# Half of the transposes, or a statistics product, placed ahead of the next product A

## What is computed

```
x = x + L0(gn(x))            # L0: a = v@Wa+ba, b = v@Wb+bb, g = sigmoid(v@Wg+bg)
                             #     per image: ab = a @ b, out = (g*ab) @ Wo + bo
x = x + L1(gn(x), filt)      # L1: stride-2 filter of a 2x dilated input, per channel:
                             #     each output is a sum of 4 taps (2x2 neighbours)
```

## Time and profile before

| | |
|---|---|
| median of 3 runs | 63.05 us |
| the profiled execution's own time | 63.02 us |
| its span, first to last instruction | 61.1 us |
| busy: TensorE products / weight loads | 47.3 / 35.8 us |
| busy: VectorE / GpSimd / ScalarE | 41.8 / 37.5 / 29.1 us |
| mean granted TensorE clock | 0.978 of full speed |

### The profile page before, as it was taken

How to read it: one execution, slowest core, us unless ns; L and a number is a source line. 1 busy time by engine, 2 the same in 40 slices (tenths; PEclk the granted TensorE clock), 3 DMA queues, 4 the chain that set the end, 5 groups by cost and what they waited for, 6 DMA issues and landing times.

```text
span 61.1 us, 2455 instructions
## 1 busy us (share of the span) xinstructions
PE 47.3 (77%) x1038; PEld 35.8 (59%) x1038; DVE 41.8 (68%) x112; ACT 29.1 (48%) x54; POOL 37.5 (61%) x51
## 2 busy tenths in 40 slices
PE   3997989877897988979979976988789895691000
PEld 3995959534865965848956835965468753330000
DVE  1076199989835675983598984588889964999700
ACT  5400003424294144657068999258891707991000
POOL 1000409449999999980572946983973996599500
PEclk9999999999999999999999999999999999999965
DMA  0899990000000000000000004040004004000494
GB/s 0 241 341 355 398 354 5 0 11 0 0 11 0 0 0 16 0 0 11 0 0 11 0 0 172 11 157 26 0 5 172 4 25 153 0 5 0 172 350 165
DMA packets 2603, 4.84 MB, mean 79 GB/s; under 512 B 288, under 2 KB 416, under 8 KB 2592
## 3 DMA queue, kind: packets, MB, share of 16 engines
q1 hardware_dynamic: 2592, 4.69, 21.3%
HBM read 2.59 MB, written 2.10 MB: 77 GB/s over the span
## 4 chain that ended last, share of the span: by engine, by line
PE 30%; DVE 17%; ACT 12%; issue 11%; POOL 10%; DVEq 2%; ACTq 0%; POOLq 0%
POOL y L250 7%; PE ps_ab L617 6%; PE ps_ot L657 5%; ACT rt L299 5%; ACT gate L312 4%; PE ps_ag L605 4%; PE ps_ot L584 4%; DVE y L449 4%; DVE part L391 3%; DVE ps_ab L464 3%; PE ps_ag L629 2%; PE ps_s L572 2%; DVEq L55 2%; PE ps_s L567 2%; PE ps_ab L641 1%
## 5 line engine op out<-in xcount | busy, mean ns | idle before, releaser
L250 POOL TENSOR_TENSOR y<-y,prod 128x512 f32<-128x512 f32 x11 | 14.0, 1274 | 5.4 <-DVE y L449 5.0
L215 POOL TENSOR_TENSOR rstd<-veps,half 128x2 f32<-128x2 f32 (+1 forms) x7 | 5.3, 759 | 11.2 <-DVE veps L419 11.2
L244 POOL TENSOR_TENSOR xb<-xs,par 128x512 f32<-128x512 f32 x8 | 8.6, 1099 | 1.6 <-issue 1.6
L559 PE MATMUL ps_ab<-zeros 128*128 128x128 f32 x54 | 8.5, 316 | 1.0 <-DVE zeros L467 1.0
L312 ACT ACTIVATE gate<-ps_ag,par 128x512 f32<-128x512 f32 x8 | 5.5, 688 | 7.5 <-PE ps_ag L629 7.5
L338 ACT ACTIVATE prod<-x,coef 128x512 f32<-128x512 f32 x11 | 7.5, 712 | 2.0 <-POOL coef L227 2.0
L559 PEld LDWEIGHTS ps_ab<-zeros 128*128 128x128 f32 x54 | 7.8, 226 | 1.0 <-DVE zeros L467 1.0
L305 ACT ACTIVATE at<-ps_ag,par 128x512 f32<-128x512 f32 x8 | 5.5, 686 | 5.6 <-PE ps_ag L605 5.6
L299 ACT ACTIVATE rt<-ps_ot 128x512 f32<-128x512 f32 x7 | 3.9, 595 | 8.7 <-PE ps_ot L584 8.7
L391 DVE BATCH_NORM_STATS2 part<-xs 128x6 f32<-128x512 f32 x8 | 5.4, 682 | 2.5 <-DMA xs<-x 2.4
L605 PE MATMUL ps_ag<-rt,par 64*64 64x256 f32 x64 | 5.3, 396 | 2.2 <-ACT gate L312 2.2
(11 more groups left out here) (59 smaller groups left out, 71.0 us busy)
## 6 DMA issues: line engine op xcount, KB each, us to landing
xs<-x SPq DMA_DIRECT2D x8, 256.0 KB, 4.3
out<-y SPq DMA_DIRECT2D x8, 256.0 KB, 2.1
par<-params SPq DMA_DIRECT2D x1, 353.0 KB, 3.5
par<-params SPq DMA_DIRECT2D x1, 128.0 KB, 2.9
```

The source lines that it names most:

```text
L244: nc.gpsimd.tensor_tensor(xb[:, w, b, :, :], xs[:, w, b, :, :], bo.broadcast_to([128, ROWS, D]), ALU.add).then_inc(xb_ready, 1)
L250: return nc.gpsimd.tensor_tensor(y[:, w, b, :, :], y[:, w, b, :, :], prod[:, n % 2, k, :, :], ALU.add)
L559: nc.tensor.matmul(bank[:, 0:128], zeros[:], zeros[:], start=True, stop=True)
```

## The change

Five edits, in the code's order:

1. GpSimd: `diag` (4 small operations for the last filter product) moves from behind `add_bo(1)` to behind `add_bo(3)`.
2. TensorE and ScalarE: in units 3 and 5 `transposes(w + 1, 0)` goes ahead of product A, and its copy ahead of `a_out`; the other half stays behind product B. It then waits for the first residual sum of the wave alone (`2 * w - 3 + n`). In units 2, 4 and 6 `stat_product(job, 0)` goes ahead of product A.
3. VectorE, prologue: `x_part(1, 0)` goes ahead of the normalisation of wave 0, `x_part(1, 1)` ahead of the copy of the first rows.
4. That copy (L483) is made in two halves, one for each unit's images, and product A(0) waits for the first half only.
5. VectorE, units 0 and 1: `deviation(1)`, `b_out(0)`, `variance(1)`, `z_out(0)`, then the statistics of waves 2 and 3; the filter's small tap operations move behind `aggregate(2)`.

```diff
--- before.py
+++ after.py
@@ -264,16 +264,16 @@
             pool.wait_ge(rstd_done, 2)
             normalise(1)
             add_bo(1)
-            pool.wait_ge(taps_ready, 1)
-            for k in range(4):
-                last = nc.gpsimd.tensor_scalar(diag[:, k, :], ident, taps[:, LAST, k:k + 1], 0.0, ALU.mult, ALU.add)
-            last.then_inc(diag_ready, 1)
             add_bo(2)
             inverse_root(2)
             pool.wait_ge(rstd_done, 3)
             normalise(2)
             normalise(3)
             add_bo(3)
+            pool.wait_ge(taps_ready, 1)
+            for k in range(4):
+                last = nc.gpsimd.tensor_scalar(diag[:, k, :], ident, taps[:, LAST, k:k + 1], 0.0, ALU.mult, ALU.add)
+            last.then_inc(diag_ready, 1)
             filter_coefs(0)
             filter_base(0)
             add_products(0, 0)
@@ -342,18 +342,22 @@
             act.wait_ge(params_in, 16)
             for g in range(UNITS):
                 w, n = divmod(g, 2)
-                a_out(g)
                 if n == 0:
+                    a_out(g)
                     if w >= 2:
                         halo_out(w - 2)
                     gate_out(g)
                     if w >= 2:
                         filter_product(w - 2, 0, 0)
                 else:
+                    if 1 <= w < LAST:
+                        transposed_out(w + 1, 0)
+                    a_out(g)
                     if w >= 2:
                         filter_product(w - 2, 0, 1)
-                    if w + 1 < WAVES:
+                    if w == 0:
                         transposed_out(w + 1, 0)
+                    if w < LAST:
                         transposed_out(w + 1, 1)
                     gate_out(g)
                     if w >= 2:
@@ -471,6 +475,7 @@
             aggregate(0)
             deviation(0)
             variance(0)
+            x_part(1, 0)
             dve.wait_ge(rstd_done, 1)
             dve.wait_ge(minus_ready, 1)
             for n in range(2):
@@ -478,31 +483,33 @@
                     last = nc.vector.tensor_scalar(gn[:, 0, 4 * n:4 * n + 4, b, :], xs[:, 0, b, 4 * n:4 * n + 4, :],
                                                    nmu[:, 0, 0, b:b + 1], rstd[:, 0, 0, b:b + 1], ALU.add, ALU.mult)
                 last.then_inc(gn0_ready, 1)
-            x_part(1, 0)
+            link(x_part(1, 1))
             dve.wait_ge(t_done, 2)
-            nc.vector.tensor_copy(rows_of(rt[:, 0, :], 1), by_image(ps_ot[:, 1, :])).then_inc(rt0_dve, 1)
-            link(x_part(1, 1))
+            for n in range(2):
+                nc.vector.tensor_copy(rows_of(rt[:, 0, :], 1)[:, 8 * n:8 * n + 8],
+                                      by_image(ps_ot[:, 1, :])[:, 8 * n:8 * n + 8]).then_inc(rt0_dve, 1)
             aggregate(1)
             x_part(2, 0)
-            deviation(1)
-            dve.wait_ge(params_in, 16)
-            for b in range(2):
-                nc.vector.tensor_copy(terms[:, :, b, 0:4].rearrange("p w (a b) -> p w a b", b=2), ftap[:, :, 1:4:2, 1:4:2])
-            nc.vector.tensor_reduce(tsum[:], ftap[:, :, 1:4:2, 1:4:2], mybir.AxisListType.XY, ALU.add).then_inc(taps_ready, 1)
-            dve.wait_ge(taps_ready, 1)
 
             for g in range(UNITS):
                 w, n = divmod(g, 2)
                 if g == 0:
+                    deviation(1)
+                    b_out(0)
                     variance(1)
-                    b_out(0)
-                    x_part(2, 1)
-                    x_part(3, 0)
                     z_out(0)
                 elif g == 1:
+                    x_part(2, 1)
+                    b_out(1)
+                    x_part(3, 0)
                     link(x_part(3, 1))
-                    b_out(1)
                     aggregate(2)
+                    dve.wait_ge(params_in, 16)
+                    for b in range(2):
+                        nc.vector.tensor_copy(terms[:, :, b, 0:4].rearrange("p w (a b) -> p w a b", b=2),
+                                              ftap[:, :, 1:4:2, 1:4:2])
+                    nc.vector.tensor_reduce(tsum[:], ftap[:, :, 1:4:2, 1:4:2], mybir.AxisListType.XY,
+                                            ALU.add).then_inc(taps_ready, 1)
                     z_out(1)
                 elif n == 0:
                     job = 2 if g == 2 else X1JOB + w - 2
@@ -578,7 +585,7 @@
                 else:
                     pe.wait_ge(gn_ready, w)
                     if w >= 2:
-                        pe.wait_ge(x1_ready, 2 * w - 2)
+                        pe.wait_ge(x1_ready, 2 * w - 3 + n)
                 for r in range(4):
 
                     last = nc.tensor.matmul(
@@ -595,8 +602,8 @@
 
             def product_a(g):
                 w = g // 2
-                if g == 0:
-                    pe.wait_ge(rt0_dve, 1)
+                if g < 2:
+                    pe.wait_ge(rt0_dve, g + 1)
                 pe.wait_ge(rt_ready, 2 * w + 1)
                 if g >= 1:
                     pe.wait_ge(gate_ready, g)
@@ -689,30 +696,33 @@
 
             for g in range(UNITS):
                 w, n = divmod(g, 2)
-                product_a(g)
                 if g == 0:
+                    product_a(g)
                     stat_product(1, 0)
                     product_b(g)
                     stat_product(1, 1)
-                    product_g(g)
-                    product_ab(g)
                 elif n == 0:
                     job = 2 if g == 2 else X1JOB + w - 2
                     stat_product(job, 0)
+                    product_a(g)
                     if w >= 2:
                         halo(w - 2)
                     product_b(g)
                     stat_product(job, 1)
                     product_o(w - 1)
-                    product_g(g)
-                    product_ab(g)
-                else:
+                elif g == 1 or w == LAST:
+                    product_a(g)
                     product_b(g)
-                    if w + 1 < WAVES:
+                    if g == 1:
                         transposes(w + 1, 0)
                         transposes(w + 1, 1)
-                    product_g(g)
-                    product_ab(g)
+                else:
+                    transposes(w + 1, 0)
+                    product_a(g)
+                    product_b(g)
+                    transposes(w + 1, 1)
+                product_g(g)
+                product_ab(g)
             idle_products(2, ps_ot[:, 0, :])
             product_o(LAST)
             stat_product(X1JOB + LAST - 1, 0)
```

## The result

The changed kernel took 64.84 us (median of 4 runs, 64.33 to 65.11), the kernel before 63.18 in the same company. The ratio of the two is 1.027 (95% interval 1.017 to 1.038): slower by 1.7 us, where 62.9 and no change were forecast. That it is slower is clear of noise; whether by more than 2% is not. Its profiled execution took 64.33 us with a span of 62.5.

The account below looks back on a forecast made before the run. The kernel was taken as bound by a ladder of hand-overs, no engine holding over 30%. The start's gain is spent by unit 3 (+0.08), unit 5 gives -0.20: sum -0.12 from 63.02, so 62.9, range 62.5 to 63.2.

Parts of the forecast that it names:

- Units 0 and 1: Early units: VectorE's tap operations take 0.33, z_out(1) starts at 17.93, B(2) loads at 18.67, -0.94.
- the late landing: Prologue rival: x_part(1, 0) waits for late data and blocks VectorE's normalisation; 64.3 if landing at 8.4; chance 0.03.
- Prologue: Start of the kernel: A(0) at 10.48, bound by idle products; squares' product, gate(0) and A(1) shift by -0.34.
- normalisation later than 7.7: Sign that the forecast is wrong: VectorE's normalisation in the prologue starts later than 7.7.
- Unit 3: A(3) waits behind transposes that need normalise(2), loading at 23.33, +0.27; start's whole gain spent by halo(0), +0.08.
- Unit 4: A(4) waits for aggregate(3) behind the means' product, loading at 27.24, before 26.95; halo(0) +0.08, which stays.
- Units 5 and 6: A copy fills ScalarE's 0.25 idle ahead of at(5), -0.20; unit 6's halo waits for filter_right, so -0.20 passes on.
- handed on: Rival at unit 3: normalise(2) does not hold up A(3), so the start's gain lives, 61.8; part or whole, chance 0.23.

Follow-up runs that it names:

- e2: The changed kernel with GpSimd's add_bo(2) moved behind normalise(3), VectorE's list untouched; 0.9935 of before, 62.84 us.
- e1: The changed kernel with VectorE's two tap copies and their sum moved from behind aggregate(2) to ahead of deviation(1); 0.995 of before, 63.33 us.
- e9: The changed kernel with each of GpSimd's add_bo operations cut in four, VectorE's list untouched; 1.015 of before, 64.38 us.
- e3: The changed kernel with each of the two tap copies replaced by a two-input addition of zeros at the same place; 1.033 of before, 65.24 us.
- e4: e1 with the order of TensorE and ScalarE of before (transposes both behind B, means' product behind A); 0.9915 of before.
- e5: e1 with both transposes of unit 3 behind B again, split in unit 5 alone; 0.986 of before.
- e6: e1 with the means' product of unit 4 behind A(4) again; 0.9875 of before.
- e8: e5 with no half of the transposes ahead of A in unit 5 either; 0.988 of before.
- e7: e5 with the prologue's statistics in the order of before: x_part(1, 0) behind wave 0's normalisation, x_part(1, 1) behind the copy; 0.988 of before.
- e10: The kernel before with only the tap copies and sum moved behind aggregate(2) and diag behind add_bo(3); 0.998 of before.

## Why the prediction was wrong

**The step that failed** is in "Units 0 and 1": "aggregate(2) about 17.25 to 17.60, tap operations 0.33, free at 17.93". 0.33 was their duration in the trace of before, taken over to a place where GpSimd is busy. They took 2.03 for the copies, 1.8 more than before, and z_out(1) starts 1.72 later than in e2, which differs in GpSimd's order alone (9.10 against 7.38 from A(0)). At halo(1) it is still 1.70 (27.75 against 26.05), and by time the two kernels stand at 1.027 and 0.9935 of before, 2.1 us apart. The term's size in the trace, 1.7, is shown by e1 and e2, and e9 moves it with the length of GpSimd's operations; the remaining 0.4 lies within the intervals, and e3 shows one thing that could fill it, a clock that falls behind such a wait. That this happened in the changed kernel's timed runs is not shown.

The prediction walked past it once: of diag it said that GpSimd "could start at once, where before it was busy" and "otherwise it is hidden". diag was costed on GpSimd alone, and what it and the joined row do to VectorE's operations beside them was not asked. The Trainium skill states the rule in "GPSIMD Engine Reference", section "Key points": GpSimd shares its SBUF interfaces with VectorE and contends with VectorE operations in a two-port mode or with two SBUF inputs. The traces agree for two SBUF inputs (2.05 us in e3) and show the same for the copy (2.03 in the changed kernel), though no trace says in which mode the copy ran. They add the size: up to the end of the operation in flight, once for each VectorE operation. In the list of rivals, slower by over 2% had 0.03, on the late landing alone.

**Prologue.** Right in that A(0) is bound by the idle products: they end at 10.82 and A(0) loads at 10.95, though the first half was in at 10.65. The gain expected there was under 0.11. The late landing was taken too lightly, from one row of one execution. 4.0 us was the shortest of the twelve traces, whose landings for this transfer reach 5.6; the wait for data in the changed kernel was 0.33, in e4 0.86. It was a matter of 0.6 to 0.7 us at most in these traces (e4, and e9, where the normalisation starts 0.67 behind the rstd), not of 2%. The sign "normalisation later than 7.7" came true in the changed kernel, at 8.05, but root(0), which ended at 7.98, had started 0.34 later than before ahead of any reordered operation; the landing added 0.04.

**Units 0 and 1, the rest.** Right: in e2 B(2) loads 8.13 behind A(0), predicted 8.19; the transposes of wave 1 wait for normalise(1), as forecast.

**Unit 3.** Right in mechanism: A(3) stands behind transposes that wait for normalise(2), and TensorE's loads idle 1.12 us in the changed kernel (0.54 and 0.61 by the forecast); e5 shows the price at A(3), 1.17 (0.61 and 0.60 by the forecast). Wrong in one size: B behind A was put at 0.62, from a row in which a 128x128 product followed. For such a product it holds (A(4) to the halo, 0.59 in the changed kernel); for B with z_out ready it is 0.27 (25.35 to 25.62). That is the main reason why e2 reaches A(4) at 16.43, not 16.76. At halo(1) e2 keeps 0.54 of the start's gain, where the forecast leaves 0.01; the other part of this is unit 5's, below. Nothing of A(3)'s weights was in early: loads and products both start at 25.35, behind the transposes.

**Unit 4.** Right: A(4) waits for aggregate(3) behind the means' product (idle 0.78, released by VectorE), worth 0.29 in e6.

**Units 5 and 6.** Right in kind: ScalarE's gap is filled, the halo still waits for filter_right (0.34 left of 0.48). The half was worth 0.36 at halo(1) (e5 and e8), not 0.20, but at halo(2) nothing of it is to be seen behind the stop in product AB(6), and by time nothing either.

**The rival "handed on"** did not come true as it was put, since normalise(2) does hold A(3). Kernel e5 takes that wait away by its order, and the early gain lives: 1.44 at halo(1) from A(0), where 1.13 was forecast (1.24 less the 0.11 of A(0) itself), and 1.4% by time. e5 has the lowest ratio of all that ran, and beats both kernels; e6, e7 and e8 are within its interval.

## What to carry to other kernels

When an operation of VectorE is moved, ask what GpSimd does at its new place, and when one of GpSimd is moved, ask which of its idle stretches, in which VectorE worked undisturbed, it closes: a tiny SBUF-to-SBUF copy can cost a whole GpSimd operation, so its duration in the old trace is good only for the old neighbour. Ahead of an engine's queue put work that is ready then; here one piece that was not ready cost 0.90 of 1.44 us. A row's spacing between two groups holds a wait if a wait stands in it, so take a pace from a place where the second group was ready.

## What was not expected of the hardware

- A VectorE copy of 16 elements a partition took 0.17 us with GpSimd idle and up to 1.13 us beside a GpSimd operation of 1.10; two-input additions the same. Of the forms that ran beside GpSimd's add_bo, BN_STATS (0.68), b_out (0.69, one input from PSUM), the copies out of PSUM (0.42 each) and the small sum over the same taps, SBUF to SBUF (TENSOR_REDUCE, 0.17 in e10), were not held. GpSimd lost nothing: its row is 4.25 us with the held copies (changed, e10) and 4.25 without (e1).
- Behind a wait of TensorE of 2.1 us the granted clock stayed at 1.00 in the changed kernel's trace and fell to the lower level in e3's, and behind one of 1.96 us in e9's.
- The transfer of x for wave 1, image 0 landed between 4.0 and 5.6 us after its issue in twelve traces of nearly the same program.
